# A decoder layer on one core: all QKV weights in SBUF from the start, and the last output projection inside the branches of the mask flag

## The reference

```python
# self-attention, 16 heads of 64; make_fxp truncates to 1/4096
qkv = jnp.einsum('bnd,ed->bne', x, w_qkv)             # w_qkv: 3072 x 128
q, k, v = (make_fxp(tohd(q)), make_fxp(tohd(k)), make_fxp(tohd(v)))
dots = make_fxp(jnp.einsum('bhnd,bhmd->bhnm', q, k) * scale)
attn = make_fxp(jax.nn.softmax(dots, axis=-1))
out = make_fxp(jnp.einsum('bhnm,bhmd->bhnd', attn, v))
out = make_fxp(jnp.einsum('bne,de->bnd', out, w_proj) + b_proj)
# cross-attention, 16 heads of 8, on a context of 1601 rows; keys = values = ctx
scores = jnp.einsum('bhqd,bhkd->bhqk', qh, kh) + encoder_attention_mask
ctx = jnp.einsum('bhqk,bhkd->bhqd', softmax(scores), vh)
x = x + jax.nn.relu(ctx @ wo_w.T + wo_b)
# feed-forward: the best 2 of 8 experts for each token
x = x + sum over the two experts of weight * ((g * sigmoid(g) * l) @ W3 + b3)
```

## Time and profile before

| | us |
|---|---|
| median of 3 runs | 715.03 |
| the runs | 709.02, 715.03, 716.03 |
| time of the profiled execution | 713.96 |
| its span | 712.2 |
| PE busy | 567.6 (80%) |
| DVE busy | 500.5 (70%) |
| ACT busy | 474.0 (67%) |
| POOL busy | 140.7 (20%) |

### The profile page before, as it was taken

How to read it: one execution, slowest core, us unless ns; L and a number is a source line. 1 busy time by engine, 2 the same in 40 slices (tenths; PEclk the granted TensorE clock), 3 DMA queues, 4 the chain that set the end, 5 groups by cost and what they waited for, 6 DMA issues and landing times.

```text
span 712.2 us, 13937 instructions
## 1 busy us (share of the span) xinstructions
PE 567.6 (80%) x5108; PEld 315.4 (44%) x5115; DVE 500.5 (70%) x896; ACT 474.0 (67%) x834; POOL 140.7 (20%) x215
## 2 busy tenths in 40 slices
PE   5798933896886856999988998899896894599992
PEld 3455511553554733333333333333332232599992
DVE  2679831884889897798888887788885522667662
ACT  3888842886889313787867886787674772577760
POOL 5000110000000352431115201230003106223332
PEclk9999985997999976999999999999997777599995
DMA  9530775077053822701091107200005001111113
GB/s 232 169 116 1 205 237 98 1 187 235 16 199 111 229 29 93 237 2 48 1 212 45 48 2 168 89 2 1 2 2 180 2 1 48 37 30 44 41 33 96
DMA packets 31717, 62.89 MB, mean 88 GB/s; under 512 B 4574, under 2 KB 21386, under 8 KB 31204
## 3 DMA queue, kind: packets, MB, share of 16 engines
q0 software_dynamic: 8000, 40.91, 21.2%
q1 hardware_dynamic: 22068, 20.31, 9.9%
q10 hardware_dynamic: 1584, 0.79, 0.4%
HBM read 42.29 MB, written 19.30 MB: 86 GB/s over the span
## 4 chain that ended last, share of the span: by engine, by line
PE 46%; DVE 21%; DMA 12%; ACT 9%; issue 6%; SPq 6%; POOLq 0%; POOL 0%; ACTq 0%; DVEq 0%
DVE smax L1688 12%; PE pair L1102 11%; PE pair L1077 6%; DMA wnat<-in_L_attn_w_qkv 6%; PE pair L1263 6%; SPq L578 4%; PE pair L1032 4%; PE pair L1251 3%; ACT region_p L1442 2%; PE pair L884 2%; ACT region_p L1343 2%; DVE region_p L1591 2%; PE pair L903 2%; PE pair L919 1%; PE pair L932 1%
## 5 line engine op out<-in xcount | busy, mean ns | idle before, releaser
L1688 DVE TENSOR_REDUCE smax<-pair 128x2 f32<-128x1024 f32 x192 | 225.5, 1219 | 54.2 <-PE pair L1032 53.5
L1442 ACT ACTIVATE region_p<-pair 128x1024 f32<-128x1024 f32 (+3 forms) x277 | 217.6, 811 | 68.2 <-PE pair L1077 62.8
L1561 DVE SCALAR_TENSOR_TENSOR region_p<-region_p 128x1024 int16<-128x1024 int16 (+1 forms) x56 | 67.1, 1220 | 9.4 <-ACT region_p L1329 7.9
L1102 PE MATMUL pair<-region_p 128*32 128x256 f32 (+1 forms) x832 | 70.0, 410 | 1.3 <-issue 1.0
L1102 PE MATMUL pair<-region_p,region_b 128*32 128x256 f32 (+1 forms) x832 | 66.5, 391 | 0.4 <-ACT region_p L1449 0.4
L1077 PE MATMUL pair<-region_b,region_k 59*128 59x256 bf16 (+1 forms) x416 | 54.7, 273 | 9.0 <-ACT region_p L1442 3.9
L1032 PE MATMUL pair<-region_k,region_b 56*128 56x512 bf16 (+1 forms) x256 | 44.3, 364 | 16.9 <-DVE smax L1688 15.7
L1343 ACT ACTIVATE region_p<-region_p 128x256 f32<-128x256 int16 x128 | 51.4, 411 | 0.0
L919 PE MATMUL pair<-ident,region_p 128*128 128x128 f32 x256 | 34.7, 279 | 16.2 <-DVE region_p L1594 16.2
L1263 PE MATMUL pair<-region_p 128*128 128x128 f32 x368 | 46.1, 280 | 0.0
L1263 PEld LDWEIGHTS pair<-region_p 128*128 128x128 f32 x368 | 44.2, 197 | 0.0
(11 more groups left out here) (244 smaller groups left out, 975.1 us busy)
## 6 DMA issues: line engine op xcount, KB each, us to landing
kimg<-region_k SPq DMA_DIRECT2D x56, 200.1 KB
region_k<-kimg POOLq DMA_DIRECT2D x8, 1400.9 KB, 15.0
region_b<-in_mask_Bx1xSxS_ff POOLq DMA_DIRECT2D x12, 800.5 KB, 8.5
region_p<-in_mask_Bx1xSxS_ff POOLq DMA_DIRECT2D x4, 800.5 KB, 13.1
region_k<-in_L_ffn_W POOLq DMA_DIRECT2D x3, 1024.0 KB, 9.4
xdisp<-region_x POOLq DMA_DIRECT2D x1, 2322.0 KB, 20.2
region_b<-in_ctx SPq DMA_DIRECT2D x3, 768.0 KB
xdisp<-region_x POOLq DMA_DIRECT2D x1, 2257.5 KB, 23.3
```

What stands on the lines that cost most here:

```text
L1102: last = pe.matmul(pair[3][32 * h:32 * h + 32, 512 + s % 2 * S:512 + (s % 2 + 1) * S], v_heads[b % 2][0:rows, t, c:c + 32], pT[0:rows, n / ...
L1442: act.activation(pT[0:rows, first // 3 % 2, k:k + size], home[0:rows, 0:size], ACT.Exp).then_inc(expt_made, 1)
L1561: return dve.scalar_tensor_tensor(out_, floor16, 0.0, floor16, ALU.is_lt, ALU.add)
L1688: last = dve.tensor_reduce(units[:, :, c // 3, c % 3], both, AX.X, ALU.max)
```

## The change

- `wnat` is no tile of its own any more but the first 3072 words of `region_k` for all eight pairs, the place in which the even half of `kstack` comes to lie later. SP issues the weights of pair 0 where it did, those of pair 1 ahead of the second context, and those of pairs 2 to 7 in three DMAs (one for q, k and v each, 128 x 6 x 128) behind the second, third and fourth context. No load of weights waits for a transpose. Pairs 2 to 7 wait for all three DMAs (`wnat_loaded[2]` at 48).
- What writes the even half of `kstack` has to wait for the eighth `w_T`: `ones_load(0)` moves on SP behind all four image stores, and the two `keys_load(0, a)` on POOL from the turns u = 3 and 4 of the loop to its last, u = 6, behind the probe load of that turn. The second half of `pads_store` moves from u = 2 to u = 3.
- On PE the last batch's three pieces and the biases' transposes (`last_finish`) stand within each branch of the flag, ahead of the unconditional branch.

```diff
-        wnat = sb("wnat", [128, 3, D])
...
+        wnat = region_k[:, 0:HP * 3 * D].rearrange("p (h c d) -> p h c d", h=HP, c=3)
...
-        w_rows = w_qkv.rearrange("(c e) d -> e c d", c=3)
+        w_rows = w_qkv.rearrange("(c h e) d -> e h c d", c=3, h=HP)
...
-            sp.dma_start(wnat[:, :, :], w_rows[0:128, :, :]).then_inc(wnat_loaded, 16)
+            sp.dma_start(wnat[:, 0, :, :], w_rows[:, 0, :, :]).then_inc(wnat_loaded[0], 16)
...
+            sp.dma_start(wnat[:, 1, :, :], w_rows[:, 1, :, :]).then_inc(wnat_loaded[1], 16)
             for k in range(1, B):
                 ctx_load(sp, CTX_ORDER[k], ctx_home[k], ctx_loaded[k])
-
-            def weights_load(hp):
-                sp.wait_ge(w_T, hp)
-                sp.dma_start(wnat[:, :, :], w_rows[bass.ds(hp * 128, 128), :, :]).then_inc(wnat_loaded, 16)
+                sp.dma_start(wnat[:, 2:HP, k - 1, :], w_rows[:, 2:HP, k - 1, :]).then_inc(wnat_loaded[2], 16)
...
-            weights_load(1)
-            image_store(0)
+            for k in range(B):
+                image_store(k)
             sp.wait_ge(ones_made, 1)
+            sp.wait_ge(w_T, HP)
             ones_load(0)
-            for k in range(1, B):
-                weights_load(2 * k)
-                weights_load(2 * k + 1)
-                image_store(k)
...
-                if u in (1, 2):
+                if u in (1, 3):
                     pads_store(0, PADS // 2) if u == 1 else pads_store(PADS // 2, PADS)
-                if u in (3, 4):
+                if u == NT - 2:
+                    pool.wait_ge(w_T, HP)
                     pool.wait_ge(kimg_written[0], 224)
-                    keys_load(0, u - 3)
+                    for a in range(2):
+                        keys_load(0, a)
...
-                pe.wait_ge(wnat_loaded, 16 * (hp + 1))
+                pe.wait_ge(wnat_loaded[min(hp, 2)], 48 if hp >= 2 else 16)
...
-                    last = pe.transpose(pair[3][:, c * 128:(c + 1) * 128], wnat[:, c, :], ident[:, :])
+                    last = pe.transpose(pair[3][:, c * 128:(c + 1) * 128], wnat[:, hp, c, :], ident[:, :])
...
+            def last_finish():
+
+                finish_tiles(B - 1, 0, pair[2])
+                finish_tiles(B - 1, 1, pair[3][:, 0:256])
+                biases_T()
+                finish_tiles(B - 1, 2, pair[3][:, 256:512])
+
+            pe.wait_ge(flag_made, 1)
+            flag = pe.value_load(mask_flag[0:1, :].bitcast(U32))
+            with pe.If(flag == 0):
+                cross_attention(False)
+                last_finish()
+            with pe.Else():
+                cross_attention(True)
+                last_finish()
```

More of the change, by code:

```diff
@@ L390, in decoder_layer @@
         ctx_loaded = [sem(f"ctx_loaded_{k}") for k in range(B)]
-        wnat_loaded = sem("wnat_loaded")
+        wnat_loaded = [sem("wnat_loaded_0"), sem("wnat_loaded_1"), sem("wnat_loaded_later")]
         mask_loaded = [sem("mask_loaded_0"), sem("mask_loaded_1")]
@@ L1188, in totals @@
                 last.then_inc(total_mm, 1)
[L1190 to L1195, removed]
             def biases_T():
```

## The result

The changed kernel takes 689.89 us in the median of 4 runs (688.10 to 692.48), the kernel before 712.12 (709.02 to 716.03): ratio 0.969, 95% interval 0.962 to 0.976. Forecast were 678.0 with a range of 670 to 688. So the change gives 22 us of the 37 forecast. A later set of runs has 688.27 against 715.66, a gain of 27 us, ratio 0.963 (0.958 to 0.968). Medians here are of all runs and ratios of the fast ones, which leaves out three of the 13 runs of before behind the median 709.83 and one of the four with the keys late, the profiled one. The profiled execution has a span of 686.3 us (time 688.10) against 712.2 before.

A forecast was written before the change was run, and what follows sets the result against it. PE's waits for weights loads queued behind image stores were taken to bound self-attention. Waits 28.9, slow clock 5.1 and branch 3.0 sum to 37.0 us, so 715.03 becomes 678.0, range 670 to 688.

The forecast's parts named there:

- the keys of the first batch: Keys loads moved to POOL's last turn: masks behind them land at 247.4, before 248.4; cost 0, high bound 20 us.
- the slow clock behind the waits: PE's pairs after the two weights waits run longer at 1.2 GHz; gain 5.1 us, bounds 5.1 and 5.9.
- the branch: End of cross-attention: a 5.5 us jump moves behind the projection, 2.5 stay visible; gain 3.0 us, bounds 0 and 5.5.
- The waits, 28.88: PE's two waits before L871 for the load of wnat, 22.63 and 6.25 us, go entirely.
- Weights in time, image and padding stores: 0: Early weights land after 29 us, needed at 49.99; nobody waits for the later image or padding stores; cost 0.
- its wait on `w_T` is over by then: Eighth transpose at 196.84 precedes POOL's probe issue at 219.24, so the new waits, also ones_load(0)'s on SP, are over.
- over 2 us there as a sign that it is wrong: Start of cross-attention: DVE waiting for mask_loaded over 2 us would show the prediction wrong.
- Rival C: Start of cross-attention: keys and masks late, DVE held up waiting for the mask; 10 us lost, 688 us; chance 0.11.
- rival D: End of cross-attention: jump hidden whole, less idle time before the half-clock stretch; 3 to 5 us less, 671 to 675; chance 0.07.
- rival B: End of cross-attention: jump only moves, DVE gets the projection's semaphore 5.5 us late; gain 34.0, 681 us; chance 0.22.

The follow-up runs named there:

- the keys late: Changed kernel with weights in oT's rows and the first ones_load early, keys of batch 0 still in the last turn: 684.29 us against 709.83, ratio 0.961.
- part 2 alone: Kernel before with only the last batch's finish moved inside both branches, weights and keys as before: 709.29 us against 709.83, ratio 0.9994.
- part 1 alone: Changed kernel with the finish behind the branch as before, so only the weights and keys changes: 687.82 us against 709.83, ratio 0.968.
- the other home: Changed kernel with weights in oT's rows, keys of batch 0 and first ones_load early as before: 683.99 us, ratio 0.964; later 683.97, ratio 0.959.
- the milder move: Kernel with weights in oT's rows, early keys and ones, plus gates and ranks one and two events earlier: 683.43 us against 715.66, ratio 0.957.

## Why the prediction was wrong

The step that failed most is the term for the keys of the first batch, "cost 0 with 1 us to spare": it cost 6.1 us, because the transfers beside them were left out. Two more terms were too large, the slow clock behind the waits (5.14, measured 2.2) and the branch (3.0, measured 0.2).

Three profiles of the code of before (its two, and the one with part 2 alone up to the branch) and three with the new weights (the changed kernel twice, and part 1 alone), us:

| stretch | before | changed | mean gain | forecast |
|---|---|---|---|---|
| start to third pair | 49.99, 50.14, 52.92 | 51.24, 53.24, 51.77 | -1.1 | 0 |
| third to eighth pair | 146.85, 146.80, 142.70 | 115.25, 115.26, 115.26 | 30.2 | 34.0 |
| eighth pair to first maxima | 61.5, 62.4, 62.5 | 68.1, 68.3, 68.1 | -6.1 | 0 |
| first maxima to group 15 end | 315.8, 320.7, 320.5 | 320.2, 321.7, 320.4 | -1.7 | 0 |
| group 15 end to first block | 39.04, 33.31 | 33.03, 33.21 | 3.1; 0.2 without the first | 3.0 |
| first block to end of DVE's last row | 93.1, 94.0 | 92.7, 92.8 | 0.8 | 0 |

With 0.2 in the fifth row the gains sum to 22.3 us; the medians of the first set of runs have 22.2, those of the later set 27.4.

- **The waits, 28.88.** Right as a mechanism: L868, which L871 has become, waits nowhere in the changed kernel. As a size they depend on the start: 28.9, 29.7 and 25.8 us in the three profiles of before. The weights land at a time that DMA sets (118.3, 119.0 and 118.1 are the starts of the row behind the long wait), so an execution that reaches the third pair late waits less. See the next point.
- **The start, not in the forecast.** At 33 us PE's rows either are and stay at full clock (L919 1.07 us, as in the first profile of before) or fall to half, from this row on or, in two profiles, from the next:

```profile
32.90 1.94 PE L916 MATMUL pair<-ident,region_p 128*128 128x128 f32 x8 [2.92 <-DVE region_p L1594]
34.77 1.67 PE L900 MATMUL pair<-region_p 64*128 64x256 f32 x8
```

 The pause ahead is 2.92 or 2.93 us in every profile. The spell costs 1.2 to 3.2 us. It is met in 9 of the 10 profiles with the new weights and in 1 of 3 without, and goes either way in the same code ahead, so a chance is likely, but whether the change makes it likelier stays open. Before, the wait for the weights absorbed it; now it is on the path. The Trainium skill, "TensorE: Matmul & The Clock Gate", section "What's actually happening", says that the window of the clock gate runs freely and that the same kernel measures differently by its phase. The trace agrees so far as the same pause of 2.92 us is followed by full clock in 3 of 13 profiles and by half in 10; the phase itself no run shows.
- **The slow clock behind the waits, 5.14.** Mis-sized: the yardstick of 22.10 us was the pair without a mask probe ahead on ACT. In the changed kernel's two later pairs of this kind ACT's `weights_move` comes after the probe, and PE waits for it with full clock too (before, ACT did the probe while PE waited for the weights):

```profile
98.99 1.98 PE L881 MATMUL pair<-xnT,wT 128*128 128x512 f32 x4 [0.73 <-ACT wT L1323]
```

 Such a pair takes 23.26 us. Against it the pairs behind the waits lost 2.8, 2.0 and 1.9 us together in the three profiles of before, 2.2 in the mean.
- **Weights in time, image and padding stores: 0.** Right: PE, ACT and DVE wait for none of them.
- **The keys of the first batch, "cost 0 with 1 us to spare".** This is the step that failed most, 6.1 us. It was called the tightest place, but only the probe, the keys and the masks were put on the queue. By that sum the masks land at 247.4 in the old count, 217.5 in the changed kernel's (29.9 less). This is just where 13 of the 16 increments of the second mask are in (217.7); the last three make it 224.7. `ones_load`, on SP, moved too, was dismissed with "its wait on `w_T` is over by then", and stands with all four pieces just where the keys now start. DVE waits for it 3.9 us, ahead of the masks, and then 4.0 for the masks; the prediction had named over 2 us there as a sign that it is wrong. Rival C had the right place and DVE as the one held up, at 10 us with the chance 0.11, but by the masks alone.
- **The branch, 3.0.** Wrong three ways. The 5.55 us were one execution's. The jump's pause is 3.2 to 3.5 us, and it is hidden whole behind the projection (0.60 and 3.14), as in rival D; the late semaphore of rival B did not come in either profile of the changed kernel. But the first block was bound by POOL's dispatch already: 12 row stores at 1.27 us, 19.7 us from the first to L1237. So nothing is gained: 0.2 us in the profiles, ratio 0.9994 alone. The rule of the Trainium skill, "Runtime: NRT & Kernel Launch", section "Instruction fetch mechanics", that execution goes on only when the target page is fetched, agrees with PE's pause in all four profiles; in the three later ones nothing ahead of the branch was late.
- **The cross-attention, 0.** The losses of the first comparison (3.2 us between first maxima and last product) are there between the two profiles of before as well (315.8 against 320.7). The first profile met fewer spells of low clock there. In the fifth and sixth group it has 22.5 and 17.0 us between moves, like one profile of the other home (22.3 and 17.0), while all others have 23.2 to 24.4 and 18.1 to 18.6; so it is no mark of the kernel before. That it looked like a usual run in its total, 713.96, came from two chances that cancel: 4.9 us won there, some 5.7 lost at the branch.

Together: 6.1 (keys and ones) + 3.8 (waits and slow clock: 34.0 - 30.2) + 1.1 (start) + 2.8 (branch) + 1.7 (spells) - 0.8 (end) = 14.7 us, the gap between 37.0 and 22.3. This account is of single profiles and closes no better than they scatter: the 1.7 rests on the first profile of before alone, which the fifth row leaves out; left out there too, the term is 0.2 and the sum of gains 23.9. The result lies 1.9 us above the range, whose end was set by rival C alone; no case in it had two terms too high at once. The lower end was called the middle of rival D; D was given as 671 to 675, and 678 less 2.5 less 3 to 5 is 670.5 to 672.5.

## What to carry to other kernels

When a load is moved, list every transfer of all queues that is in flight at its new place, with the small ones first: a copy into three partitions beside 2.8 MB of another queue took 27 us instead of 8 to 9, held up two engines, and the masks behind those keys ended late too. Put data that is loaded early into a place that is written late (here each weight into its own head pair's output row), and no other load has to move. A row that stands once in one execution, such as a held increment or a pair's length, is a term only after a second profile; and before a pause is counted as a gain, look whether the next transfer's chain ends just behind it.

## What the runs showed of the hardware

A taken branch over a long body held up PE for 3.2 to 3.5 us and, in the one pair of profiles without a cover, cost 4.2, of which 2.6 are pause. ACT, released by the product ahead of it, once started 5.55 us after that product's end, and 0.07 us after it in three other profiles, for a reason that stays open. A copy of 75 KB into three partitions beside 2.8 MB of another queue took 25 to 27 us, and of the 16 increments of the masks behind that queue's keys three came up to 8 us behind the others. Moving three steps of routing by 1 to 3 events in the last group went with a granted clock of 0.61 instead of 0.90 in both runs with it (21.5 us against 16.9), and not with the milder move (0.87, 17.8 us); which of the moved steps does it was not tried.
